# Grouped convolution as three products per phase pair instead of four, and a reordered prologue

## The reference, cut to what matters

```
x: (32, 64, 1024)  cond: (32, 128)  bias: (64,)
weight: (64, 16, 9)   c_weight: (64, 128)   kernel: (1024, 1024) bool   scale: scalar
y = conv1d(x, weight, stride 1, padding 4, groups 4)      # along the last axis, 9 taps
y = y + (cond @ c_weight.T)[:, :, None] + bias[None, :, None]
w = kernel * 2.0 - 1.0                                    # +1 or -1
out = x + scale * (y @ w)                                 # over the last axis, 1024 by 1024
```

## Time and profile before

| | |
|---|---|
| median of 3 runs | 180.75 us |
| profiled execution | 180.59 us |
| its span | 178.8 us |
| TensorE busy | 171.2 us, 96% |
| VectorE busy | 127.5 us, 71% |
| ScalarE busy | 68.1 us, 38% |
| GpSimd busy | 7.4 us, 4% |
| granted TensorE clock, mean | 0.99 |

### The profile page before, as it was taken

The page is one execution under the profiler, slowest core; times in us unless marked ns, Lnnn a source line. Parts: engine busy times, 40 slices in busy tenths (PEclk is TensorE's granted clock), DMA queues, the critical chain, the costliest instruction groups (busy, mean ns, idle before and its releaser), DMA issues.

```text
span 178.8 us, 2874 instructions
## 1 busy us (share of the span) xinstructions
PE 171.2 (96%) x1010; PEld 147.5 (83%) x1010; DVE 127.5 (71%) x188; ACT 68.1 (38%) x77; POOL 7.4 (4%) x18
## 2 busy tenths in 40 slices
PE   7699999999999999999999999999999999998991
PEld 2379888898989889988989898988998898986781
DVE  5736466979996877687675967596766877587662
ACT  3203993566452543329071634237061502042000
POOL 4230600000000000000000000000000000000000
PEclk9969999999999999999999999999999999999999
DMA  5589697768886792776757793778463650005006
GB/s 216 132 152 279 206 262 188 186 105 207 192 283 164 104 343 47 109 167 125 283 84 175 116 318 56 130 146 204 192 96 55 90 233 0 2 0 235 4 0 235
DMA packets 23629, 27.35 MB, mean 153 GB/s; under 512 B 2752, under 2 KB 19072, under 8 KB 23616
## 3 DMA queue, kind: packets, MB, share of 16 engines
q1 hardware_dynamic: 22176, 25.63, 56.8%
q0 software_dynamic: 368, 1.07, 2.4%
q10 hardware_dynamic: 1072, 0.48, 1.3%
HBM read 10.32 MB, written 8.40 MB: 105 GB/s over the span
## 4 chain that ended last, share of the span: by engine, by line
PE 93%; DMA 2%; DVE 1%; ACTq 1%; issue 0%; DVEq 0%
PE ps_conv L658 33%; PE ps_A L681 28%; PE ps_C L681 14%; PE ps_B L681 7%; DMA taps_nat<-weight 2%; PE ps_B L698 2%; PE ps_A L698 2%; PE ps_toep L698 2%; PE ps_C L698 2%; PE ps_toep L681 1%; PE ps_toep L636 1%; PE ps_C L647 1%; DVE sums L214 1%; PE ps_A L624 1%; DVE x_nat L513 0%
## 5 line engine op out<-in xcount | busy, mean ns | idle before, releaser
L658 PEld LDWEIGHTS ps_conv<-toeplitz,x_blk 128*128 128x128 f32 x512 | 60.4, 194 | 2.6 <-issue 0.8
L658 PE MATMUL ps_conv<-toeplitz,x_blk 128*128 128x128 f32 x512 | 60.8, 278 | 0.0
L475 DVE TENSOR_TENSOR y_sum<-ps_conv,shift 128x512 f32<-128x512 f32 (+1 forms) x33 | 22.2, 674 | 17.4 <-PE ps_conv L658 12.4
L373 ACT CAST hi_S<-sums 128x512 fp32r<-128x512 f32 x28 | 16.6, 620 | 43.4 <-DVE sums L492 42.7
L373 ACT CAST hi_A<-y_sum 128x512 fp32r<-128x512 f32 x24 | 14.0, 616 | 41.5 <-DVE y_sum L475 41.5
L358 ACT COPY x_phase<-x_nat 128x1032 f32<-128x1032 f32 x13 | 28.3, 2177 | 3.0 <-DMA x_nat<-x 3.0
L513 DVE SCALAR_TENSOR_TENSOR x_nat<-ps_A,scale_col,x_nat 128x512 f32<-128x512 f32 x27 | 20.3, 750 | 11.2 <-PE ps_A L681 11.2
L502 DVE TENSOR_TENSOR lo_S<-sums,hi_S 128x512 fp32r<-128x512 f32 x28 | 19.0, 680 | 0.0
L502 DVE TENSOR_TENSOR lo_A<-y_sum,hi_A 128x512 fp32r<-128x512 f32 x24 | 16.3, 682 | 1.7 <-ACT hi_A L373 1.7
L681 PE MATMUL ps_A<-sign_T,hi_S 128*128 128x512 f32 x56 | 16.2, 412 | 1.1 <-DVE x_nat L513 0.9
L681 PE MATMUL ps_A<-sign_T,lo_S 128*128 128x512 f32 x56 | 15.0, 389 | 0.0
(11 more groups left out here) (104 smaller groups left out, 174.3 us busy)
## 6 DMA issues: line engine op xcount, KB each, us to landing
x_nat<-x SPq DMA_DIRECT2D x16, 512.0 KB, 4.2
out<-x_nat SPq DMA_DIRECT2D x15, 512.0 KB, 4.8
x_blk<-x_phase SPq DMA_DIRECT2D x118, 64.5 KB, 2.5
w_bytes<-w_bool SPq DMA_DIRECT2D x2, 512.0 KB, 6.3
shift<-shift_dram POOLq DMA_DIRECT2D x1, 768.0 KB, 6.1
x_blk<-x_phase ACTq DMA_DIRECT2D x6, 64.5 KB, 3.7
x_blk<-x_phase POOLq DMA_DIRECT2D x4, 64.5 KB, 3.0
out<-x_nat SPq DMA_DIRECT2D x1, 256.0 KB, 2.9
```

The lines of the kernel that those rows point to most:

```text
L373: nc.scalar.copy(hi[k][:, :, :], flat(operand(k))).then_inc(hi_ok[k], 1)
L475: nc.vector.tensor_tensor(y_sum[r][:, u, a, :].rearrange("m u a o -> m a u o"), ps_conv[:, a, u, :], shift_of(d, r, a).unsqueeze(2).to_bro ...
L658: now = nc.tensor.matmul(ps_conv[:, a].rearrange("m u o -> m (u o)"), x_blk[r][:, a, s:s + M], toeplitz[:, s, g].rearrange("r u o -> r u ( ...
```

## The change

**Three products from double 2 on.** With x_e the blocks at even m offset and x_o those at odd, GpSimd makes two differences per pair, `dif[0] = x[0::2] - x[1::2]` and `dif[1] = x[1::2] - x[2::2]` (128 by 512 each, `differences`), ScalarE copies `odd = x[1::2]` (`odd_blocks`, 128 by 512). TensorE does three products per group g over both images: odd with the sum of the two Toeplitz matrices, dif[0] with the first, dif[1] with the second. Twelve products per pair in place of sixteen. VectorE makes the results, three instructions per pair in place of two (`fast_y`): uneven = middle + shift, even = first + uneven, uneven = uneven - third. These lie by parity of m and image; four DMAs of 128 KB per pair, issued by ScalarE's queue (`to_parity`), bring them into `y_sum`. VectorE makes the sum of the Toeplitz matrices once. The set for pair 1 lies over `w_bytes`.

**Order.** Both convolutions of d+1 stand behind P1. The low and high parts are merged into groups: A (A11, A12), S12, S34 in one instruction of twice the length each, A22 alone. S3 and S4 of a double are made at the start of its own step. `x_nat` has 12 slots in place of 16 pairs; loads of doubles 6 and 7 wait for stores. The shift is kept per pair and channel, loaded by two broadcast DMAs.

**Prologue.** Taps are issued first on ScalarE's queue; GpSimd spreads the second half of them, before its block DMAs; the small transposes stand between the two halves of the tap transposes; the phase copy of pair 1 comes earlier on VectorE. Warm-up is 11 and 2, the 2 ahead of the wait for the small operands. conv(0, r) waits block by block, in the order in which they are issued. The first load of w stands ahead of pair 1's block DMAs on SyncE's queue.

```diff
+WARM = 11, 2
+FIRST_ORDER = [[a for (of, half), blocks in FIRST_BLOCKS.items() if half == h for a in blocks] for h in range(2)]
 # GpSimd
+            pool.wait_ge(taps_in, 16)
+            expand_taps(nc.gpsimd.tensor_copy, KH, B).then_inc(exp_ok, 1)
             first_blocks(pool, "POOL", 0)
...
+            def differences(d, r):
+                if d > 2:
+                    pool.wait_ge(m_done[0], order(d - 1, r) + 1)
+                    pool.wait_ge(m_done[2], order(d - 1, r) + 1)
...
+                for h in range(2):
+                    wait_blocks(pool, d, r, h)
+                for e in range(2):
+                    nc.gpsimd.tensor_tensor(dif[r][:, e], x_blk[r][:, :, e:e + M:2], x_blk[r][:, :, e + 1:e + 1 + M:2][:, :, 0:K],
+                                            ALU.subtract).then_inc(dif_ok[r], 1)
 # ScalarE
+            act.dma_start(taps_nat[:, :, :], weight).then_inc(taps_in, 16)
             act.dma_start(cond_nat[:, :], cond).then_inc(small_in, 16)
             act.dma_start(cw_nat[:, :], c_weight).then_inc(small_in, 16)
-            act.dma_start(taps_nat[:, :, :], weight).then_inc(taps_in, 16)
...
+                nc.scalar.copy(odd[r], x_blk[r][:, :, 1:1 + M:2]).then_inc(odd_ok[r], 1)
...
+                for p, made in ((0, y_even_ok), (1, y_odd_ok)):
+                    act.wait_ge(made, order(d, r) + 1)
+                    for i in range(2):
+                        act.dma_start(y_sum[r][p::2, i], y_two[r][i * K:(i + 1) * K, p]).then_inc(y_in[r], 16)
...
             def step(d):
-                for k in ("S3", "S4", "A22"):
-                    high_part(k, d)
+                high_part("S34", d)
+                if runs(d, 2):
+                    odd_blocks(d + 1, 1)
+                high_part("A22", d)
                 if runs(d, 4):
                     to_phases(d + 2, 0)
-                if runs(d, 2):
-                    high_part("A12", d + 1)
-                    high_part("A11", d + 1)
-                if runs(d, 4):
                     to_phases(d + 2, 1)
                 if runs(d, 2):
-                    high_part("S1", d + 1)
-                    high_part("S2", d + 1)
+                    to_parity(d + 1, 0)
+                    to_parity(d + 1, 1)
+                if runs(d, 4):
+                    odd_blocks(d + 2, 0)
+                if runs(d, 2):
+                    high_part("A", d + 1)
+                    high_part("S12", d + 1)
 # VectorE
+            def fast_y(d, r):
...
+                nc.vector.tensor_tensor(uneven, ps_conv[:, 1],
+                                        shift[:, 2 * d + r].rearrange("m (g o) -> m g o", g=GROUPS).unsqueeze(2)
+                                        .to_broadcast([P, GROUPS, B, CG]), ALU.add).then_inc(mid_ok, 1)
...
+                nc.vector.tensor_tensor(even, ps_conv[:, 0], uneven, ALU.add).then_inc(y_even_ok, 1)
+                nc.vector.tensor_tensor(uneven, uneven, ps_conv[:, 2], ALU.subtract).then_inc(y_odd_ok, 1)
...
             def step(d):
                 if d > 1:
                     sum_up("C21_A", d - 1)
-                    low_part("S2", d)
+                    combine("S3", d)
+                    combine("S4", d)
                 sum_up("C11_P2", d)
-                low_part("S1", d)
                 sum_up("C11_P1", d)
-                low_part("S3", d)
+                if d > 1:
+                    low_part("S12", d)
                 if runs(d, 2):
-                    add_shift(d + 1, 0, 0)
-                low_part("S4", d)
+                    fast_y(d + 1, 0)
+                low_part("A22", d)
                 if runs(d, 2):
-                    add_shift(d + 1, 0, 1)
-                low_part("A22", d)
+                    fast_y(d + 1, 1)
                 sum_up("C12_A", d)
...
+                low_part("S34", d)
                 sum_up("C22_C", d)
...
                 sum_up("C22_A", d)
...
+                    low_part("A", d + 1)
+                    combine("S1", d + 1)
+                    sum_up("C12_C", d)
                     combine("S2", d + 1)
-                    sum_up("C12_C", d)
-                    combine("S4", d + 1)
 # TensorE
+            def fast_conv(d, r):
...
+                for m, taps, read in ((1, 2, mid_ok), (0, 0, y_even_ok), (2, 1, y_odd_ok)):
+                    if n:
+                        pe.wait_ge(read, n)
...
+                    for g in range(GROUPS):
+                        both = slice(2 * g, 2 * g + 2)
+                        of = odd[r][:, both] if m == 1 else dif[r][:, m // 2, both]
+                        now = nc.tensor.matmul(ps_conv[:, m, g].rearrange("m u o -> m (u o)"),
+                                               of.rearrange("r b k -> r (b k)"),
+                                               toeplitz[:, taps, g].rearrange("r u o -> r (u o)"), start=True, stop=True)
+                    now.then_inc(m_done[m], 1)
...
                 if runs(d, 2):
-                    conv(d + 1, 0)
+                    fast_conv(d + 1, 0)
+                    fast_conv(d + 1, 1)
                 product("P6", d, bank["A"], False, False, "C11_P1", 1)
                 product("P5", d, bank["C"], True, False, "C12_C")
-                if runs(d, 2):
-                    conv(d + 1, 1)
```

More of the change, by code:

```diff
@@ L66 @@
 PLAIN_DONE = {"A": 5, "B": 6, "C": 7, "E": 8}
[L67 removed]
+OPERANDS = "A11", "A12", "S1", "S2", "S3", "S4", "A22"
+SPLITS = {"A": ("A11", "A12"), "S12": ("S1", "S2"), "S34": ("S3", "S4"), "A22": ("A22",)}
+SPLIT_OF = {k: of for of, ks in SPLITS.items() for k in ks}
 PRODUCTS = "P1", "P2", "P3", "P4", "P5", "P6", "P7"
@@ L172, in last, with order @@
             return d == DOUBLES - 1
[L174 to L179, removed]
-            else:
-                eng.wait_ge(blk_in[r][h], 16 * GROUPS * d)
+        def order(d, r):
+            return 2 * (d - 2) + r
         def line(d, r, lo_, hi_):
-            return x_nat[:, 2 * d + r, lo_:hi_]
+            return x_nat[:, (2 * d + r) % SLOTS, lo_:hi_]
         def row(ap, d, r):
@@ L294, in _ @@
                 step(d)
-            sp.wait_ge(stored, 16 * (PAIRS + 2))
+            for j in range(PAIRS - 1):
+                sp.wait_ge(stored[j], 16)
+            sp.wait_ge(stored[PAIRS - 1], 16 * 3)
         @block.gpsimd
@@ L367, in high_part, with high_0 @@
+            def high_0(k):
+                act.wait_ge(y_ok, 3 if k == "A12" else 4 * int(k[1]))
+                nc.scalar.copy(images(hi[k]), operand(k)).then_inc(hi_0[k], 1)
+            def high_part(k, d):
+                if k in ("S12", "S34"):
+                    for part in SPLITS[k]:
+                        act.wait_ge(s_ok[part], d)
+                elif d == 1:
+                    act.wait_ge(y_ok, 12 if k == "A" else 16)
                 else:
-                    act.wait_ge(y_ok, 8 * d + 4 * int(k[1]))
+                    act.wait_ge(y_in[0 if k == "A" else 1], 16 * 4 * (d - 1))
@@ L369, in high_part @@
                 if d > 1:
-                    act.wait_ge(done[PRODUCT_OF[k]], d - 1)
-                elif d == 1 and k not in ("S1", "S2", "S3"):
-                    act.wait_ge(plain_done, LAST_USE["A21" if k == "S4" else k])
-                nc.scalar.copy(hi[k][:, :, :], flat(operand(k))).then_inc(hi_ok[k], 1)
+                    for part in SPLITS[k]:
+                        act.wait_ge(done[PRODUCT_OF[part]], d - 1)
+                else:
+                    act.wait_ge(plain_done, {"A": 6, "S12": 1, "S34": 8, "A22": 4}[k])
```

312 lines of the change are left out of this document (192 added, 120 removed).

## The result

The changed kernel takes 192.24 us (median of four runs, 190.95 to 193.03), the kernel before 180.72 beside it: ratio 1.063 [1.056, 1.070]. The forecast was 175.0 with a range of 168.5 to 186. It was wrong in direction and in range. Profiled execution: 192.94 us, span 191.1. The medians are over all executions, and the ratios leave out those more than 1.5% above their kernel's fastest, as the ones in the profiles of e4, e5 and e12 are; the two part where a kernel's executions spread, as in e5 (174.86 to 179.78 us) and e12 (178.3 to 182.13).

What follows compares the result with a forecast made beforehand. TensorE was taken to bound the kernel before. Span 178.8 - 1.25 (prologue) - 1.15 (step 1) - 3.85 (steps 2 to 6) + 0.5 (last step) = 173.05, with time around it 175.0 us; range 168.5 to 186.

Steps and rivals of the forecast that it cites:

- steps 2 to 6: Five doubles: each falls from 19.87 to the loop's 19.1 us, 0.77 less, 3.85 in all.
- The convolution: TensorE, per pair: 24 records in 2.68 us for 32 in 3.57; 1.79 less per double, which alone would last 18.05.
- The loop: Chain past TensorE from one S4 to the next, through ScalarE, block DMAs and VectorE: 19.1 us per double.
- SyncE's branch: Middle of the loop: eight block DMAs issued in 5.05 us, the last landing 1.9 later, 6.95 together; loop 18.65.
- ScalarE's branch: Middle of the loop: phase copy of pair 1, 2.17, then eight y DMA issues, 5.2: 7.4 us, 0.45 more than SyncE's.
- rival 1: GpSimd's differences hold VectorE's low part of A, S3 and S4: +1.2 to +2.35 us per double, 181 to 187; chance 0.32.
- Rivals 1 and 2: Rival 1, GpSimd's hold, chance 0.32; rival 2, DMAs crowd issues and landings: +1.2 us in five steps, 181, chance 0.16.
- Step 1: First step after double 0: second pair's convolution waits 1.0 us for VectorE; 19.1 in place of 20.26, 1.15 less.
- The prologue: Taps issued 1.0 us earlier, spreading shared with GpSimd, first convolution at about 9.0: -1.25, bounds 0 and -3.
- which the block-by-block order hides: Prologue: GpSimd's block DMAs go out up to 0.4 us later, at no cost to the first convolution.
- the half clock: First convolution in the prologue, at the 1.2 GHz level before: 0.25 us counted as won, -3 bound at full clock throughout.
- The last step: Keeps its work; P1 waits some 0.5 us for C21_A, as in the loop: +0.5.

Runs made afterwards that it cites:

- e4: The changed kernel with each y DMA moving an eighth of its bytes, as many DMAs (y not computed); median 8.4 us less than the changed kernel.
- e5: The changed kernel with both GpSimd's differences cut to one block of eight and y DMAs to an eighth; median 14.6 us less than the changed kernel.
- e12: The kernel of e7 with all differences on VectorE instead of GpSimd, low S12 behind the first y instructions; 180.26 us, 0.990 of the kernel before.
- e3: The changed kernel with GpSimd's differences cut to one block of eight (convolution not computed); median 6.6 us less than the changed kernel.
- e1: The changed kernel with the whole prologue of the kernel before; 4.3% slower than the kernel before.
- e9: The kernel before with the change's prologue, first w load behind pair 1's block DMAs, warm-ups 13 and 6 for 11 and 2; 1.002 of before.
- e7: e1 with ScalarE's high part of S34 moved last and, in step 1, VectorE's last sign sums behind the y instructions; 182.47 us.
- e2: The kernel before with the whole prologue of the changed kernel; 182.78 us, 0.8% slower than the kernel before.

## Why the prediction was wrong

The forecast span was 173.05, the measured one 191.1. Of the 18.05 between them 7.35 lie in steps 2 to 6 (+3.5 in place of -3.85), 5.75 in step 1 and 4.95 in the prologue.

**The convolution, right in its records, short in what it saves.** 24 records, 2.74 against 2.68. But a double without any wait takes TensorE 18.57, not 18.05 (e5). The loop is longer and hid it; alone it would have cost 0.5 per double.

**The loop, right in shape, wrong in its terms.** From one S4 to the next (94.56 to 116.10 in the trace after) are 21.5 us; forecast were 19.1. The same distance is 21.5, 19.8 and 21.6 in the other doubles. Up to the end of pair 0's phase copy 4.2 went (forecast 4.6). From there to `odd` 9.0 went (98.78 to 107.79), where I had put 6.95 for SyncE's branch and 7.4 for ScalarE's: this step of the sum was mis-sized, at 5.05 + 1.9, with the issue rate and landing of a queue that issues alone. ScalarE's branch was not the bound, since its queue issued the y DMAs while its copy ran (98.68 and 99.14 in the queues' fence); that term was wrong in kind, and the 0.45 that it added to the forecast had no ground. From `odd` to S4 8.3 went (forecast 6.9), and the 1.4 more are the holds that rival 1 had priced at 1.2 to 2.35.

**Rivals 1 and 2 are not alternatives.** The step that failed is the one from the rivals to the numbers: I gave the hold 0.32 and the DMAs 0.16 as if one or the other could be, and the forecast none of either. Both are set off by the same change, both lie in the same loop, and e3, e4 and e5 show both. The sum had to hold them together: 18.65 + 1.2 (hold, its lower end) + 2.05 (issues and landing, as measured above) = 21.9, against 21.5 in this double. The prediction's own prices would have done, 19.1 + 1.2 + 1.2 = 21.5, where the mean of steps 3 to 6 is 21.06. The Trainium skill, page "SBUF — State Buffer", section "Who interferes with whom", had the rule for the hold: one side fully blocks until the other's instruction ends. The trace agrees (S3 1.51, S4 1.53, each longer by 0.8, where 0.96 and 0.99 of a difference were left). The absence of a row with two SBUF operands beside GpSimd was no evidence against it, and I had used it so.

**Step 1: +4.6 in place of -1.15.** I took before's time of the sign sums. In the trace after, they come behind S1 and S2, held while pair 0's differences run, and behind the low part of S12, and are themselves held (windows with the granted clock below; here VectorE and GpSimd):

```profile
44.05 2.50 POOL L402 TENSOR_TENSOR set<-x_blk 128x512 f32<-128x512 f32 x2 [23.68 <-DMA x_blk<-x_phase]
44.35 1.29 DVE L623 TENSOR_TENSOR sums<-y_sum 128x512 f32<-128x512 f32 x1
45.75 1.35 DVE L623 TENSOR_TENSOR sums<-sums,y_sum 128x512 f32<-128x512 f32 x1
...
50.02 3.19 DVE L561 TENSOR_TENSOR sign_T<-sign_B,sign_T 128x1024 fp32r<-128x1024 f32 x2
...
50.77 3.35 POOL L402 TENSOR_TENSOR w_bytes<-x_blk 128x512 f32<-128x512 f32 x2 [4.22 <-DMA x_blk<-x_phase]
...
54.64 0.68 DVE L597 TENSOR_TENSOR y_two<-ps_conv,shift 128x512 f32<-128x512 f32 x1
```

S1 and S2 cost 1.3 more, the sign sums 0.84 (3.19 against 2.35 in the earlier trace rows). TensorE waits 3.52, not 1.0, and the convolution after the gap takes 5.45 for 2.94, at the 1.2 GHz level (0.50 in the window 55 to 60). How much of this falls in step 1 depends on when the prologue ends: e1, with the same lists in it, has the sign sums at 2.35, waits 2.62 and takes 21.27. e4 has the same gap, 3.53, with the convolution behind it at 2.94, and its step is 2.5 shorter: that is the clock's share.

**The prologue: +3.7 in place of -1.25.** The taps came earlier, and the last transposes too, but the first convolution started at 10.15, after 1.09 of waiting for a block, not at 9.0 (9.98 in before). My line "which the block-by-block order hides" failed: 4.8 in place of 3.7 for a landing was on the path and ate the gain of the taps. The rest is the clock. The windows (length, busy time of PE, PEld, DVE, ACT, POOL, granted clock, DMA share, GB/s) show it at its lower level past 19 us:

```profile
9.00:14.00 5.00, 3.91 (x15) 3.13 (x14) 0.91 (x3) 0.00 (x0) 0.85 (x2) 0.55 0.97 234
14.00:19.00 5.00, 5.00 (x21) 4.01 (x20) 1.38 (x2) 1.91 (x1) 1.67 (x1) 0.50 0.93 321
55.00:60.00 5.00, 4.62 (x21) 4.62 (x22) 3.59 (x6) 0.86 (x1) 0.00 (x0) 0.50 0.78 155
```

The kernel before and then e4 had it in full in the second of these windows:

```profile
14.00:19.00 5.00, 5.00 (x46) 5.00 (x46) 3.43 (x6) 2.58 (x5) 0.55 (x1) 1.00 0.95 313
```

```profile
14.00:19.00 5.00, 5.00 (x46) 5.00 (x47) 3.36 (x6) 3.80 (x3) 1.35 (x1) 1.00 1.00 334
```

I had counted the half clock as a thing the change could only shorten (0.25 won, at best 3). It cuts both ways: four kernels with the same prologue (after, e3, e4, e5) reach P2 of step 1 at 45.14, 44.13, 41.75 and 45.00, and e4 alone had the clock back by 14 us. Against it, after loses 3.4 of the 3.7; 0.2 of that is its later first convolution (10.15, 9.92 in e4), and the rest is the clock, which differed between executions of the same instructions. Only e9 changed the clock on purpose. What the last 0.3 are, no run separates.

**The last step** cost 0.5, the number of the forecast but by luck: P1 doesn't wait there. The one wait of TensorE in it, 0.94 behind P1, stands in before too, and the products are longer, 0.93 for four matmuls in place of 0.905 to 0.92.

## What to carry to other kernels

When a change adds work on GpSimd and DMAs to a loop that has no slack, price every VectorE instruction with two SBUF operands at its length plus the remainder of GpSimd's, price DMA issues and landings by rows in which two queues issue at once, and add these up: they are one case, not two rivals. Here the same arithmetic on VectorE, which is the busier engine, gave a median of 180.26 in e12 against 182.47 on GpSimd in e7, 1.2% less, with one more instruction moved. TensorE work removed (10.7 us counted here, 7.8 by the doubles without a wait) is worth nothing before the longest loop that avoids TensorE is shorter than what remains; and a wait put into a prologue can cost the clock as well.

## What had not been expected of the hardware

- A VectorE copy from SBUF to SBUF (the taps' spreading, one operand) took 1.48 in place of 0.68 while GpSimd's copy of the same shape ran from 4.57 to 6.05. It ended 0.55 after that, as S3 did after the first difference:

```profile
4.57 1.48 POOL L250 COPY sums<-taps_nat 64x576 f32<-64x576 f32 x1 [1.07 <-DMA taps_nat<-weight]
...
5.12 1.48 DVE L250 COPY sums<-taps_nat 64x576 f32<-64x576 f32 x1
```

So not only two-operand instructions are held, which the prediction's reading of the rule had left out. The y instructions, with one operand in PSUM, were never longer than 0.69.
- ScalarE's sequencer issues DMAs while its engine executes a copy: 0.47 for the first at 98.65, with a copy from 98.68 to 100.78.
- A GpSimd difference of 512 columns at a stride of two takes 1.03 alone, half of the copy's 2.19 for 1032; its second operand cost nothing that shows.
- The clock after a gap of 3.5 us was low in one run of the same instructions (5.45 for 24 records) and full in another (2.94). After a gap of 2.34 in e12 it was low too (4.46), after 2.62 in e1 full (2.94).
- The clock column can say 1.00 over matmuls that run at the pace of the lower level (e2, 2.93 for twelve records; 1.58 in e9). The durations of like records are the surer sign.
